# Low-pass convolution block on one core: x read twice and block-transposed by VectorE, filtered rows moved to columns inside SBUF

## The reference, cut to what matters

```
xs  = gelu(einsum('bhwc,dc->bhwd', x, W1) + b1)      # 768 -> 192 channels
xs  = |real(ifft2(mask * fft2(xs)))|                 # low-pass over h and w, each channel
xs  = einsum('bhwd,cd->bhwc', xs, W2) + b2           # 192 -> 768 channels
out = x + xs
```

## Time and profile before

| | |
|---|---|
| median of 3 runs | 2677.9 us |
| profiled execution, first to last instruction | 2680.7 us |
| mean granted TensorE clock | 0.975 of full |
| PE busy | 2549.4 us (95%) |
| DVE busy | 1833.9 us (68%) |
| ACT busy | 1350.4 us (50%) |
| POOL busy | 397.9 us (15%) |
| moved by DMA | 509.48 MB, mean 190 GB/s |

### The profile page before, as it was taken

How to read it: one execution, slowest core, us unless ns; L and a number is a source line. 1 busy time by engine, 2 the same in 40 slices (tenths; PEclk the granted TensorE clock), 3 DMA queues, 4 the chain that set the end, 5 groups by cost and what they waited for, 6 DMA issues and landing times.

```text
span 2680.7 us, 53277 instructions
## 1 busy us (share of the span) xinstructions
PE 2549.4 (95%) x16864; PEld 2485.4 (93%) x16864; DVE 1833.9 (68%) x3980; ACT 1350.4 (50%) x3077; POOL 397.9 (15%) x500
## 2 busy tenths in 40 slices
PE   8899898998999989899998999989999899998999
PEld 7799898998989989899898999989999899998999
DVE  6487575775758757587675766757667576675767
ACT  5355454554545545455454545545455454554544
POOL 1102021020211202112020120201202012020120
PEclk9899999999999999999999999999999999999999
DMA  6474664746647466474665846558455584555845
GB/s 207 106 252 138 201 242 114 264 129 200 240 114 261 131 198 242 114 273 129 204 230 129 282 116 215 208 135 298 103 211 202 140 300 99 207 204 145 299 102 221
DMA packets 342566, 509.48 MB, mean 190 GB/s; under 512 B 78418, under 2 KB 210770, under 8 KB 342228
## 3 DMA queue, kind: packets, MB, share of 16 engines
q1 hardware_dynamic: 342228, 505.31, 59.8%
HBM read 253.60 MB, written 251.66 MB: 188 GB/s over the span
## 4 chain that ended last, share of the span: by engine, by line
PE 83%; DMA 6%; SPq 4%; issue 3%; DVE 2%; ACT 2%; DVEq 0%; ACTq 0%
PE ps L400 22%; PE ps L385 12%; PE ps L401 10%; PE ps L472 6%; PE ps L462 6%; PE ps L463 5%; PE ps L469 5%; PE ps L466 5%; DMA xt_hi<-filtered_rows 4%; PE ps L437 3%; SPq L317 2%; PE ps L411 2%; PE ps L445 2%; DMA filtered_rows<-filt 2%; PE ps L413 2%
## 5 line engine op out<-in xcount | busy, mean ns | idle before, releaser
L400 PE MATMUL ps<-w1s,xt_hi 128*128 128x384 f32 x3072 | 980.2, 374 | 0.0
L521 ACT ACTIVATE xt_hi<-ps 128x512 fp32r<-128x512 f32 x768 | 457.7, 598 | 697.8 <-PE ps L385 674.5
L401 PE MATMUL ps<-w1s,xt_lo 128*128 128x192 f32 x3072 | 772.3, 251 | 0.0
L640 DVE TENSOR_TENSOR xt_lo<-ps,xt_hi 128x512 fp32r<-128x512 f32 x768 | 529.8, 691 | 282.4 <-ACT xt_hi L521 279.6
L702 DVE TENSOR_TENSOR xs<-ps,xs 128x384 f32<-128x384 f32 x1024 | 564.5, 556 | 210.9 <-PE ps L472 159.8
L401 PEld LDWEIGHTS ps<-w1s,xt_lo 128*128 128x128 f32 x3072 | 588.0, 191 | 0.0
L400 PEld LDWEIGHTS ps<-w1s,xt_hi 128*128 128x128 f32 x3072 | 578.8, 188 | 0.0
L472 PE MATMUL ps<-w2b_hi,ob 128*128 128x384 f32 x1024 | 357.0, 349 | 42.7 <-DVE ob L693 42.7
L763 POOL TENSOR_TENSOR diff<-hid 128x192 f32<-128x192 f32 x240 | 232.2, 967 | 1016.8 <-ACT hid L529 1016.8
L462 PE MATMUL ps<-w2a_hi,oa_hi 128*128 128x384 f32 x1024 | 361.3, 353 | 20.8 <-DVE xs L702 19.7
L385 PE MATMUL ps<-ident,xs 128*128 128x128 f32 x2304 | 344.1, 273 | 11.2 <-DMA xs<-x_dram 10.6
(11 more groups left out here) (62 smaller groups left out, 3051.3 us busy)
## 6 DMA issues: line engine op xcount, KB each, us to landing
out_dram<-xs SPq DMA_DIRECT2D x127, 1536.0 KB, 9.3
xs<-x_dram SPq DMA_DIRECT2D x80, 1536.0 KB, 7.2
filtered_rows<-filt SPq DMA_DIRECT2D x256, 192.0 KB, 2.0
x_tail<-x_dram SPq DMA_DIRECT2D x32, 1536.0 KB, 8.5
xs<-x_dram SPq DMA_DIRECT2D x32, 768.0 KB, 6.3
xt_hi<-filtered_rows SPq DMA_DIRECT2D x64, 256.0 KB, 5.1
cols_b<-filtered_rows SPq DMA_DIRECT2D x128, 128.0 KB, 5.4
xt_lo<-filtered_rows SPq DMA_DIRECT2D x64, 256.0 KB, 6.4
```

The lines of the kernel that those rows point to most:

```text
L400: nc.tensor.matmul(ps_h[t % 2][:, 0:2 * D], hi, w1s[:, k, :], start=k == 0, stop=False)
L401: ins = nc.tensor.matmul(ps_h[t % 2][:, D:2 * D], lo, w1s[:, k, 0:D], start=False, stop=k == KC - 1)
L521: nc.scalar.activation(xt_hi[:, n % XT_SLOTS, :], ps_xt[n % 2][:], ACT.Copy).then_inc(s_xhi, 1)
L640: nc.vector.tensor_tensor(xt_lo[:, n % XT_SLOTS, :], ps_xt[n % 2][:], xt_hi[:, n % XT_SLOTS, :].bitcast(F32), ALU.subtract).then_inc(s_xlo, 1)
```

## The change

Every engine's program is rewritten around tiles of 128 pixels and pairs of them.

- x is read twice. For the first half SP loads each pair into `xq` in an order by which 32x32 blocks can be turned in place, with four transfers of 32 partitions each (`load_xq`). For the final sum it loads the pair again, pixels on partitions, into a ring of eight pairs, `xr` (`load_xr`). There is no `xs`.
- TensorE's transposes, the identity and their PSUM banks are gone. VectorE transposes each tile in SBUF, 768 columns in blocks of 32x32 (`transpose_tile`). ScalarE's hi and VectorE's lo read that SBUF tile (768 columns to an instruction) and write it in TensorE's order; W1 is laid out to match.
- The DRAM tensor is gone. After each pair's filter along w, SP moves `filt` to `cols_a` and `cols_b`, which lie in SBUF for the whole image, with 24 transfers a pair, each to one partition (`scatter_rows`). `filt` has four places in place of two. A place is free again when its 24 transfers have landed.
- The lo parts of gelu and of `ya` move from VectorE to GpSimd. All 12 absolute values of filter H move to ScalarE. VectorE's bias sums take a pair and its final sum a whole tile in one instruction.
- The order is new. The first half runs `LEAD` = 3 pairs ahead of the second half of the image before, pair by pair; three pairs of the next image stand between the banks of filter H. SP's list has the scatter of a pair, the loads and the store in the same order.

```diff
-            def write_rows(i, q):
-                sp.wait_ge(s_fs, PAIRS * i + q + 1)
-                sp.dma_start(rows_in[:, 2 * q:2 * q + 2, :], filt[:, q % 2, :, :]).then_inc(s_fw[q % 2], 16)
+            def load_xq(i, p):
+                if p >= XQ or later(i):
+                    sp.wait_ge(s_t, TILES * i + 2 * (p - XQ) + 2)
+                for j in range(QUADS):
+                    sp.dma_start(xq[j * B:(j + 1) * B, p % XQ, :, :].rearrange("p t (g c) -> p (t g) c", c=CQ),
+                                 x_q[i, p, :, :, j * CQ:(j + 1) * CQ]).then_inc(s_xq[p % XQ], 16)
...
+            def scatter_rows(i, q):
+                if q == 0 and later(i):
+                    sp.wait_ge(s_y, YS * i)
                 sp.wait_ge(s_fs, PAIRS * i + q + 1)
+                for t in range(2):
+                    for a in range(2):
+                        for w2 in range(2):
+                            p = w2 * H + 4 * q + 2 * t + a
+                            first = a * W + w2 * W // 2
+                            sp.dma_start(cols_a[p:p + 1, :, :], filt[first:first + W // 2, q % FILT, t, 0:P]
+                                         ).then_inc(s_cols[q % FILT], 16)
+                            for v in range(2):
+                                sp.dma_start(cols_b[p:p + 1, :, v * DB:(v + 1) * DB],
+                                             filt[first + v * BCOLS:first + (v + 1) * BCOLS, q % FILT, t, P:D]
+                                             ).then_inc(s_cols[q % FILT], 16)
...
+            def turn(i, a, c, n):
                 if a:
+                    for q in range(LEAD - 1):
+                        scatter_rows(i, q)
+                for r in range(PAIRS):
+                    q = r + LEAD
+                    if a and q < PAIRS:
+                        feed(i, q, n)
+                    if c and 3 <= r < 3 + PAIRS - XR:
+                        load_xr(i - 1, r + X_AHEAD)
+                    if c and r >= 1:
+                        store(i - 1, r - 1)
+                    if a and r >= PAIRS - X_AHEAD:
+                        load_xr(i, r - (PAIRS - X_AHEAD))
+                    if a and q <= PAIRS:
+                        scatter_rows(i, q - 1)
+                for k in range(CHUNKS):
+                    if c and k == 0:
+                        store(i - 1, PAIRS - 1)
+                    if a and k < XR - X_AHEAD:
+                        load_xr(i, X_AHEAD + k)
+                    if n and k < LEAD:
+                        feed(i + 1, k, n)
...
             def stage_filtered(i, q):
                 act.wait_ge(s_f, PAIRS * i + q + 1)
-                if q >= 2 or later(i):
-                    act.wait_ge(s_fw[q % 2], 16 * (PAIRS // 2 * i + q // 2))
+                if q >= FILT or later(i):
+                    act.wait_ge(s_cols[q % FILT], 16 * MOVES * (PAIRS // FILT * i + q // FILT))
...
+            def transpose_tile(i, t):
+                q = t // 2
+                if t % 2 == 0:
+                    dve.wait_ge(s_xq[q % XQ], 16 * QUADS * (PAIRS // XQ * i + q // XQ + 1))
+                nc.vector.transpose(xt[:, t % XT, :], xq[:, q % XQ, t % 2, :]).then_inc(s_t, 1)
```

More of the change, by code:

```diff
@@ L196, in later, with wrap @@
             return not isinstance(i, int) or i > 0
[L198 to L227, removed]
+        def wrap(i, q, n):
+            if q < PAIRS:
+                return i, q
+            return (i + 1, q - PAIRS) if n else None
         def y_slot(c, v):
@@ new lines, in _, with feed @@
+            const(w1f, w1t.rearrange("p (k d) -> p k d", d=D), s_w1)
+            load_xq(0, 0)
+            for t in range(2):
+                const(b1_rows[:, t, :], b1.partition_broadcast(P), s_b1_rows)
+            load_xq(0, 1)
+            load_constants()
+            for p in range(2, XQ):
+                load_xq(0, p)
+            for q in range(LEAD):
+                load_xq(0, q + X_AHEAD - 1)
+            def feed(i, q, n):
+                ahead = wrap(i, q + X_AHEAD - 1, n)
+                if ahead is not None:
+                    load_xq(*ahead)
@@ L361, in _ @@
+            turn(0, True, False, True)
+            with sp.Fori(1, IMAGES - 1) as i:
+                turn(i, True, True, True)
+            turn(IMAGES - 1, True, True, False)
+            turn(IMAGES, False, True, False)
+            for k in range(XR):
+                sp.wait_ge(s_out[k], 16 * 2 * IMAGES)
+            for k in range(FILT):
+                sp.wait_ge(s_cols[k], 16 * MOVES * PAIRS // FILT * IMAGES)
         @block.tensor
         def _(pe):
-            pe.wait_ge(s_ident, 16)
@@ new lines, in corner_sums, with filter_h_item @@
+                nc.tensor.matmul(ps_c[0:4, 0:D], corner_w[:], corner_acc[:], start=True, stop=True).then_inc(s_cmm, 1)
+            def filter_h_item(i, c, v):
+                k = YBANKS * c + v
+                bank = y_ring[k % len(y_ring)]
+                if k == 0:
+                    for j in range(FILT):
+                        pe.wait_ge(s_cols[j], 16 * MOVES * PAIRS // FILT * (i + 1))
+                if k == 0:
+                    pe.wait_ge(s_corner, i + 1)
+                elif k < len(y_ring):
+                    if later(i) and k % 2 == 1:
+                        pe.wait_ge(s_add, TILES * i - 1 + k // 2)
+                else:
+                    pe.wait_ge(s_yabs, YS * i + k - len(y_ring) + 1)
+                own = corner[:, 0:P] if v < 2 else corner[:, P:2 * P]
+                nc.tensor.matmul(bank, own, corner_hw[:], start=True, stop=False)
@@ new lines, in feed @@
+            def feed(i, q, n, k):
+                ahead = wrap(i, q + 1, n)
+                if ahead is not None:
+                    xt_hi_tile(ahead[0], 2 * ahead[1] + k)
+            for t in range(2):
+                xt_hi_tile(0, t)
+            for q in range(LEAD):
+                for k in range(2):
+                    feed(0, q, True, k)
+                if q >= 1:
+                    stage_filtered(0, q - 1)
+                gelu_pair(0, q)
+            set_up_at = {0: set_up_w2a_hi, 1: set_up_w2b_hi, 2: set_up_corner}
@@ new lines, in feed_transpose @@
+            def feed_transpose(i, q, n, k):
+                ahead = wrap(i, q + 2, n)
+                if ahead is not None:
+                    transpose_tile(ahead[0], 2 * ahead[1] + k)
+            dve.wait_ge(s_w1, 16)
+            link(nc.vector.tensor_copy(w1s[:, :, 0:D], w1f))
+            nc.vector.tensor_tensor(w1s[:, :, D:2 * D], w1f, w1s[:, :, 0:D].bitcast(F32), ALU.subtract).then_inc(s_w1s, 1)
+            for t in range(2):
+                transpose_tile(0, t)
+            for t in range(2):
+                xt_lo_tile(0, t)
+                transpose_tile(0, 2 + t)
@@ L770, in filters @@
+            turn(0, True, False, True)
+            with pool.Fori(1, IMAGES - 1) as i:
+                turn(i, True, True, True)
+            turn(IMAGES - 1, True, True, False)
+            turn(IMAGES, False, True, False)
 def filters():
```

685 lines of the change are left out of this document (285 added, 400 removed).

## The result

The changed kernel takes **5362.92 us** (median of four runs, 5353.46 to 5365.59) against 2675.26 for the kernel before on the same chip: a ratio of **2.003**, 95% interval 1.998 to 2.008. One of the four runs of the kernel before took 6215.89 us and is left out of the ratio; the other three took 2672.42 to 2677.90. The change is slower, as forecast, and inside the range, though near its upper end: the forecast was 4115.

A forecast was written before the change was run, and what follows sets the result against it. SP's issuing of transfers was taken as the bound: 184.3 us scatter, 28.1 `xq`, 10.3 other issues and 29.9 without scatter make 252.6 us an image; sixteen make 4042, plus 73 around them gives 4115 us, range 3100 to 5400.

The forecast's parts named there:

- TensorE's gain on offer: TensorE without transposes and the DRAM turn: 131.8 us left of an image's about 167, so 35 us to gain.
- TensorE's share: TensorE's busy share in the profile after: near half, 2109 of 4115 us.
- The engines beside it: VectorE 118 us an image, GpSimd 52 us more than its 25, ScalarE little changed; none sets the time.
- SP's list as the bound: SP issues 480 transfers an image one after the other; with the stretch without scatter, 252.6 us an image.
- The scatter's issue: SP's price for one scatter transfer: 0.48 us, so 184.3 us for an image's 384.
- the high end: Upper bound on SP's issue price, from reads by columns to 64 partitions: everything at 0.67 us, kernel 5390 us.
- The stretch without scatter: Around filter H at each image's end: last landing, banks with three pairs, and a slow start, 29.9 us an image.
- The time around the images: Before the first scatter 25 us, after the last filter H 60, less 12 for three pairs: 73 us.
- What stops the other engines: ScalarE waits before the fifth `filt` copy for a scatter to land; TensorE and VectorE then stop too.
- Rival 1: SP's small transfers are issued cheaply: at 0.20 us each the kernel takes 2280 us; chance 0.12.
- Rival 2: The scatter's landing in one partition binds, not the issue: 10.0 us a pair, kernel 3124 us; chance 0.08.
- Rival 3: Scatter pieces cost SP more than 0.67 us or back up in its queue: kernel over 5400 us; chance 0.05.

The follow-up runs named there:

- experiment 5: Changed kernel without any scatter, the filter along h computed on zeros and not waiting for landings: 2319.77 us.
- experiment 3: Changed kernel with the same 24 transfers a pair and the same runs, each run a quarter as long: 5363.42 us.
- Experiment 4: Changed kernel with ScalarE issuing the second half of each pair's scatter in place of SP: 3756.47 us.
- experiment 1: Transfers alone, nothing computed, twelve of each form in a row: an issue inside SBUF took 0.59 to 0.60 us, the write to DRAM 0.44.
- experiment 2: Changed kernel with both column tiles merged, 8 scatter transfers a pair for 24, same bytes: 3018.83 us, ratio 1.128 to the kernel before.
- experiment 9: Changed kernel with the turn through DRAM and its 16 reads put back, rest of the change kept: 2559.27 us, ratio 0.9587 to the kernel before.

## Why the prediction was right, and what was mis-sized

**TensorE's gain on offer: right, with a misread row.** 131.8 us an image were left; with the scatter taken away TensorE is busy 2183 / 16 = 136.4. A misread row accounts for most of the difference: the 0.44 us of four transposes is their duration in the chain, and by the distance of starts, as the other blocks were read, it is 0.35. From the timeline of the kernel before (start us, us, operation):

```profile
1039.93 0.60 PE L385 MATMUL ps<-ident,xs 128*128 128x128 f32 x4
...
1040.28 0.42 PE L400 MATMUL ps<-w1s,xt_hi 128*128 128x384 f32 x1
```

The pair's three groups (0.35 here, 0.36 and 0.35 for the next two) make 1.06 us in place of 1.32. That leaves 4.18 us a pair and 136.0 an image.

**TensorE's share: near half as forecast, but by luck.** Its 49% are 2628 us of 5362, not 2109 of 4115; 2109 us would be 39%. In the changed kernel it waits for half of the span at a mean granted clock of 0.732, and a product with W1's hi and lo (L272) lasts 475 ns in the mean; in experiment 5, at 94% busy and a clock of 0.968, the same one lasts 372 (L256). The forecast had priced every block at full clock. It cost no time here, since TensorE was not the bound.

**The engines beside it: right in sum, not in each term.** Groups of the changed kernel (count | busy us, mean ns | idle before):

```profile
L516 DVE STREAM_TRANSPOSE xt<-xq 128x768 f32<-128x768 f32 x512 | 497.8, 972 | 2170.1 <-DMA xq<-x_dram 2170.1
L520 DVE TENSOR_TENSOR xt_lo<-xt,xt_hi 128x768 fp32r<-128x768 f32 x512 | 576.9, 1127 | 862.9 <-ACT xt_hi L385 862.6
L635 POOL TENSOR_TENSOR hid_lo<-hid,hid_hi 128x384 fp32r<-128x384 f32 x256 | 259.1, 1012 | 4275.3 <-ACT hid L395 4275.3
L559 DVE TENSOR_TENSOR xr<-ps_o,xr 128x768 f32<-128x768 f32 x512 | 482.1, 942 | 92.9 <-PE ps_o L332 91.4
```

The block transpose takes 972 ns where the row of the same length gave 948, and the final sum 942 for 961. The lo part takes 1127, not 948. VectorE is busy 1928.1 / 16 = 120.5 us an image, for 118. GpSimd was overrated, 77 us an image for 47.4 measured: 384 columns take 1012 ns, where I had doubled the 967 of 192 columns; that row was no clean price, for the same subtraction takes 675 ns in the changed kernel; why, no run here shows. None of it sets the time.

**SP's list as the bound: right, and this was the argument that mattered.** Experiments 3, 4 and 5 leave no other: bytes do nothing, a second issuer takes 1606 us off, no scatter takes 3043 off.

The Trainium skill, page "DMA: Bandwidth & Descriptors", section "Issuing engines are not separate DMA queues", says that starting transfers from several engines saves only the sequencer's time for the start, usually small beside the transfer. Experiment 4 agrees that this time is saved; that it is small does not hold here, where a piece lands 1.8 to 2.1 us after its issue, several are under way at once, and the 384 starts of an image fill 259.5 of its 333.2 us.

**The scatter's issue: the mis-sized term.** I took 0.48 us, the distance of the small constants. Measured are 0.63 steady and 0.676 in the mean; 259.5 - 184.3 = 75.2 us an image, 93% of the 80.6 us by which the image was forecast too short. Of the 75.2, 57.6 are the steady price and 17.6 the long single issues. The nearest row was the high end, the reads by columns at 0.67, and by that end alone the range took the result in, with 37 us to spare. I judged nearness by "small, in an unbroken row", but in experiment 1 size and runs don't enter, and an unbroken row inside SBUF costs 0.59 all the same. All rows that I drew on had DRAM on one side, and none was a transfer inside SBUF.

The high end was itself added up too low: its "everything at 0.67" leaves the 24 other issues at 0.43. With them at 0.67 too it is 16 x (460 x 0.67 + 29.9) + 73, some 5480 us, above the stated range.

**The other issues: right.** `xq` at 0.54 and the rest at 0.43 gave 38.4 us; 40.9 were measured.

**The stretch without scatter: 32.9 for 29.9, with a term in it that I had not seen.** The timeline of TensorE in two such stretches (start us, us, operation, idle before):

```profile
1634.21 0.77 PE L305 MATMUL ps_c<-corner_hw,corner 128*128 128x512 f32 x1 [52.09 <-DMA cols_b<-filt]
...
1659.81 1.05 PE L308 MATMUL ps_o<-fh,cols_b 128*128 128x128 f32 x8
1665.74 0.68 PE L272 MATMUL ps_h<-w1s,xt_hi 128*128 128x384 f32 x1 [4.88 <-issue]
...
4994.61 1.05 PE L308 MATMUL ps_o<-fh,cols_b 128*128 128x128 f32 x8
```

From SP's next transfer (1633.01) to the end of the last bank (1659.81 + 1.05 = 1660.86) it is 27.9 us: the rest of the landing, then filter H with its three pairs. Then come 6.2 us, to SP's next scatter at 1667.08, in which neither SP nor TensorE (4.88) waits for anything shown; one image later this pause is 3.9 us. It comes with the repeat of the program's loop over images: each of the thirteen repeats has it, 3.8 to 6.2 us long on SP, and at the end of the first image and of the fifteenth, where the instructions go straight on into or out of the loop, there is none. The trace has the branch itself: at each of the thirteen repeats SP's next instruction starts 5.5 to 7.9 us after the branch of the loop (L253) has ended, from 1659.36 to 1666.88 here; the fourteenth time, where it goes straight on, 0.05 us after. What sticks out behind filter H is the pause. Meanwhile packets of the queues that the page's part 3 calls "instruction" (q8 and q14) start: eight to ten around the last bank's end at each repeat (5 us before to 7 after), two and none at the other two ends. The last bank shown above ended at 4995.66, and the scatter behind it started at 4995.69; these two stretches take 28.1 and 27.9 us. No row that I had read told of this pause. The 32.9 is so near the 29.9 because the terms that I had came out some 2 us shorter and the pause is some 5 us long.

**The time around the images: 31 us for 73.** The first scatter starts at 31.6 us, for 25. But the first image takes 301.7 us, 31.5 less than a later one, and from the sixteenth image's first scatter to the end it is 366.6 us, only 33 more than an image. This hid 42 us of the shortfall.

**What stops the other engines: wrong in its place.** I expected ScalarE before a `filt` copy, waiting for a place to be scattered. That wait is 9.8 us in the whole span, one time (the first row). The waits that are there (us in all, times, longest):

```profile
ACT filt L401 <- DMA cols_b<-filt: 9.8, 1, 9.8
ACT hid_hi L394 <- DVE hid L534: 2308.9, 236, 21.0
DVE xt L516 <- DMA xq<-x_dram: 2170.1, 191, 18.7
PE ps_h L272 <- DVE hid L534: 1623.9, 164, 19.0
PE ps_c L305 <- DMA cols_b<-filt: 844.9, 16, 59.3
```

VectorE's transposes wait for `xq`, because its loads stand behind the scatters of the step before in SP's list, and VectorE, TensorE and ScalarE then wait around one another. So the way back from SP's list is the input, not the places of `filt`. It changes nothing in the sum, since either way SP's list paces the pair.

**The rivals.** Rival 1, cheap issue, needed 0.266 us; nothing inside SBUF was under 0.50. Its end, TensorE at its own floor, is what experiment 5 shows (2320 for 2280). Rival 2, the landing, fell with experiment 3 as what sets this kernel's time. A pair's issues take 24 x 0.63 = 15.1 us, more than the 10.0 us that the rival gave the landing. The Trainium skill, page "SBUF — State Buffer", section on the DMA port swizzle, gives the rate of a port from which the prediction estimated 7.2 us a pair; no run here shows that limit.

Rival 3 was near in time (5400), and part of it is there. The steady distance stayed under its 0.67. But the backlog that it named fits the long single issues: of the 328 distances above 0.8 us from one scatter issue to the next in the thirteen images, 218 are among the first five after SP's loads and store. They bring the mean to 0.676.

**What is left open.** Why a transfer with 64 partitions or with one costs 0.6 us to issue and with 32 or 128 partitions of DRAM traffic 0.43; why inside SBUF the price is 0.59 in every form; how the time of experiment 2 divides between SP and the DMA engines; and whether experiment 9, with its DMA engines full, would gain by reading x once.

## What to carry to other kernels

Count the transfers before the bytes: a move that is split into many small pieces was paid for by the issuing queue here, 0.63 us each, and everything else in that queue, the next inputs first, stands behind it. When a change has two parts, price each by itself: here the rest of the change, with the transposes on VectorE, was worth 4% beside the old turn through DRAM, and the scatter in that turn's place cost a factor of two. Where an unknown price is bounded by rows, ask what the rows have in common that the new operation lacks (here DRAM on one side), before taking the middle.

## What the runs showed of the hardware that I had not expected

- In rows of twelve, the issue of a transfer inside SBUF took 0.59 to 0.60 us on SP in the median, whether it has one run of 512 B or 128 of them, one landing partition or all, and 0.61 on ScalarE's queue, which ran beside SP's without loss.
- With DRAM on one side it was 0.43 to 0.45 with 32 or 128 partitions, and 0.59 to 0.82 with one or 64. Inside a kernel it can be less: medians of 0.34 for the `xq` loads of the changed kernel and 0.36 for the write of rows before.
- A repeat of the loop over images, whose body issues 480 transfers, kept SP from its next instruction for 5.5 to 7.9 us after the branch, thirteen times; TensorE stood 4.0 to 6.3 us between the two images with no wait for another engine shown. Where the loop was left, SP went on after 0.05 us.
- GpSimd's subtraction of 192 columns took 967 ns in one kernel and 675 in the other.
